# A DLRM tower on one core: a memset behind each gather, no pause for the dots, dense features turned in the third pass, loads in a new order

## The reference

```python
e = jnp.stack([tbl_0[ids[:, 0]], ..., tbl_25[ids[:, 25]]], axis=1)      # [512, 26, 128]
combined = jnp.concatenate([dense_features[:, None, :], sparse_features], axis=1)
interactions = jnp.einsum('bnd,bmd->bnm', combined, combined)
z = jnp.concatenate([dense_features, interactions[:, _TRIU_I, _TRIU_J]], axis=1)
h = jnp.concatenate([z, r_dense_features], axis=1)                      # 607 columns
h = jnp.maximum(h @ W_top1 + b_top1, 0.0)                               # 512
h = jnp.maximum(h @ W_top2 + b_top2, 0.0)                               # 256
y = h @ W_top3
```

## Time and profile before

| what | value |
|---|---|
| median of 3 runs | 134.91 us |
| time of the profiled execution | 134.64 us |
| its span in the profile | 132.1 us |
| TensorE busy | 110.6 us (84%) |
| VectorE busy | 83.8 us (63%) |
| ScalarE busy | 77.6 us (59%) |
| GpSimd busy | 59.6 us (45%) |

### The profile page before, as it was taken

The page is one execution under the profiler, slowest core; times in us unless marked ns, Lnnn a source line. Parts: engine busy times, 40 slices in busy tenths (PEclk is TensorE's granted clock), DMA queues, the critical chain, the costliest instruction groups (busy, mean ns, idle before and its releaser), DMA issues.

```text
span 132.1 us, 2612 instructions
## 1 busy us (share of the span) xinstructions
PE 110.6 (84%) x1036; PEld 94.5 (72%) x1036; DVE 83.8 (63%) x161; ACT 77.6 (59%) x146; POOL 59.6 (45%) x57
## 2 busy tenths in 40 slices
PE   0032996999999999999999189949989997999992
PEld 0022654868888888888888099849978996899891
DVE  5422399999999998897932507954950683095101
ACT  3019972499795959598584307945960776067120
POOL 2087878879788979878778400004700000000000
PEclk9999999999999999999999855999999999999999
DMA  4999976939888785881211100000110000000000
GB/s 96 275 406 390 347 264 186 297 118 212 342 207 330 202 336 191 261 314 56 56 48 46 53 0 5 0 5 7 52 25 0 5 0 0 5 0 5 0 0 1
DMA packets 6492, 16.99 MB, mean 129 GB/s; under 512 B 1617, under 2 KB 2897, under 8 KB 6354
## 3 DMA queue, kind: packets, MB, share of 16 engines
q1 hardware_dynamic: 4274, 13.38, 29.5%
q0 software_dynamic: 1536, 3.15, 8.7%
q10 hardware_dynamic: 672, 0.32, 1.0%
HBM read 16.83 MB, written 0.00 MB: 127 GB/s over the span
## 4 chain that ended last, share of the span: by engine, by line
POOL 41%; PE 25%; issue 17%; DVE 9%; DMA 5%; ACT 2%
POOL rows L306 41%; PE dots_ps L620 8%; DVE z L324 8%; PE acc_ps L647 8%; DMA ids_sb<-ids 4%; PE turn_ps L661 3%; PE acc_ps L638 2%; PE turn_ps L593 2%; ACT z L348 1%; PE acc_ps L661 1%; PE turn_ps L671 1%; DVE cols L316 1%; PE acc_ps L671 1%; DMA rows<-tbl,ids_sb 1%; ACT h L427 0%
## 5 line engine op out<-in xcount | busy, mean ns | idle before, releaser
L306 POOL DMA_INDIRECT rows<-tbl,ids_sb x48 | 58.7, 1222 | 35.0 <-PE turn_ps L593 16.4
L465 DVE TENSOR_SCALAR onehot<-ids_row,row_number 128x1024 fp32r<-128x1024 int32 x49 | 33.2, 745 | 4.3 <-PE acc_ps L568 3.1
L324 DVE COPY z<-dots_ps 30x128 f32<-30x128 f32 (+5 forms) x80 | 21.0, 263 | 8.8 <-issue 5.6
L348 ACT ACTIVATE z<-dots_ps 30x128 f32<-30x128 f32 (+5 forms) x80 | 19.7, 246 | 11.5 <-PE dots_ps L620 10.3
L620 PE MATMUL dots_ps<-cols 128*64 128x52 f32 x512 | 18.9, 240 | 6.3 <-DMA rows<-tbl,ids_sb 3.2
L620 PEld LDWEIGHTS dots_ps<-cols 128*64 128x64 f32 x512 | 18.2, 156 | 7.5 <-issue 5.6
L560 PE MATMUL acc_ps<-onehot,table_hi 128*128 128x512 f32 x68 | 18.7, 422 | 3.1 <-ACT table_hi L348 3.1
L475 DVE TENSOR_TENSOR table_lo<-table_raw,table_hi 128x2048 fp32r<-128x2048 f32 (+1 forms) x8 | 16.6, 2079 | 4.8 <-ACT table_hi L348 4.8
L560 PEld LDWEIGHTS acc_ps<-onehot,table_hi 128*128 128x128 f32 x68 | 13.0, 200 | 8.3 <-ACT table_hi L348 4.2
L568 PE MATMUL acc_ps<-onehot,table_lo 128*128 128x512 f32 x68 | 17.4, 408 | 1.0 <-DVE table_lo L475 1.0
L348 ACT ACTIVATE cols<-turn_ps 128x512 f32<-128x512 f32 x10 | 10.6, 1082 | 10.4 <-PE turn_ps L593 10.4
(11 more groups left out here) (42 smaller groups left out, 72.0 us busy)
## 6 DMA issues: line engine op xcount, KB each, us to landing
table_raw<-picked_tables SPq DMA_DIRECT2D x14, 512.0 KB, 7.0
ids_row<-ids_picked SPq DMA_DIRECT2D x7, 512.0 KB, 5.1
table_raw<-w SPq DMA_DIRECT2D x1, 1536.0 KB, 8.4
rows<-tbl,ids_sb POOLq DMA_INDIRECT x48, 3.7
w_sb<-w SPq DMA_DIRECT2D x1, 512.0 KB, 12.5
dense_sb<-dense ACTq DMA_DIRECT2D x1, 256.0 KB, 6.8
table_raw<-picked_tables SPq DMA_DIRECT2D x2, 128.0 KB, 5.8
ids_sb<-ids ACTq DMA_DIRECT2D x1, 52.0 KB, 5.3
```

The lines of the kernel that those rows point to most:

```text
L306: nc.gpsimd.indirect_dma_start(rows[:, t % GATHER_RING, n, :], None, tables[f][:, :], index).then_inc(rows_in[t][g], 16)
L324: last = copy(z[QUAD * q:QUAD * q + rows_of, t % 2, :, QUAD * s + b0:QUAD * s + b1], src.rearrange("i b c -> i c b"))
L348: return nc.scalar.activation(dst, src, ACT.Copy)
L465: nc.vector.tensor_scalar(onehot[:, c], ids_row[:, pair % IDS_RING], row_number[first_row][:, c:c + 1], None, ALU.is_equal).then_inc(oneho ...
```

## The change

- Behind each of the 48 gathers GpSimd clears `breath`, 256 columns of 128 partitions that nobody reads. The memset of gather k waits for that of gather k-1.
- `PAUSES` and `LANDED` are empty: group (3,2) is no longer held back until the dots of tile 1 are done, and `dots(0)` waits for no landing.
- The dense features are turned between the two halves of pass 2 (`DENSE_PASS`), and their three copies stand in passes 3, 4 and 5 of ScalarE. ScalarE's first instruction on data is now `split_hi(0)`; the one-hot of pass 1 is made ahead of `split_hi(1)`.
- `dense_sb` is loaded by SP, behind the tables of pass 2, from an array laid out on the host so that a partition's data is contiguous; so is `w2`; `w3` and `b2` are one load.
- In the tiles t >= 1, group (t+2, 2) is turned behind layer 2, and moved by ScalarE behind `activate2`.

```diff
-PAUSES = {(3, 2): 1}
-LANDED_FIRST = [(3, 0), (3, 1)]
+DENSE_PASS = 2
+PAUSES = {}
+LANDED = {}
+BREATH = 256
...
-            for p in range(PASS_RING):
-                if PASSES[p][3] and PASSES[p][0] < IDS_RING:
-                    load_ids_row(PASSES[p][0])
-                load_tables(p)
-            sp.dma_start(w2_sb[:], w2.rearrange("(k p) o -> p k o", p=P)).then_inc(w2_in, 16)
-            sp.dma_start(w3_sb[:], w3).then_inc(small_in, 16)
-            sp.dma_start(b2_sb[:], b2).then_inc(small_in, 16)
+            load_ids_row(0)
+            load_tables(0)
+            load_tables(1)
+            load_ids_row(1)
+            load_tables(2)
+            sp.dma_start(dense_sb[:], dense).then_inc(dense_in, 16)
+            sp.dma_start(w2_sb[:], w2).then_inc(w2_in, 16)
+            sp.dma_start(last_sb[:], last_weights).then_inc(small_in, 16)
...
                     for n in group:
                         f = GATHERED[n]
+                        k = t * len(GATHERED) + n
                         index = bass.IndirectOffsetOnAxis(ap=ids_sb[:, t, f:f + 1].bitcast(U32), axis=0)
                         nc.gpsimd.indirect_dma_start(rows[:, t % GATHER_RING, n, :], None, tables[f][:, :],
                                                      index).then_inc(rows_in[t][g], 16)
+                        if k:
+                            pool.wait_ge(breathed, k)
+                        nc.gpsimd.memset(breath[:], 0.0).then_inc(breathed, 1)
...
-            act.wait_ge(dense_turned, 1)
-            copy(dense_t[:].rearrange("d (h e j) -> d h e j", e=2, j=QUAD),
-                 dense_turned_ps.rearrange("d (h j e) -> d h e j", e=2, j=QUAD))
-            copy(cols[:, :, 0], dense_turned_ps)
-            copy(cols[:, :, NODES + REPEATS.index(0)], dense_turned_ps).then_inc(dense_moved, 1)
             split_hi(0)
-            for p in range(NP):
-                if ACT_CHUNKS[p]:
+            measure(1)
+            finish_onehot(1)
+            split_hi(1)
+            for p in range(1, NP):
+                if p >= 2:
                     measure(p)
                 if p + 1 < NP:
                     split_hi(p + 1)
-                if ACT_CHUNKS[p]:
+                if p >= 2:
                     finish_onehot(p)
...
+                if p - DENSE_PASS in (1, 2, 3):
+                    move_dense(p - DENSE_PASS - 1)
...
                 activate1(t)
-                for g in range(2, NG):
-                    move_group(t + 2, g)
+                if t == 0:
+                    for g in range(2, NG):
+                        move_group(t + 2, g)
                 if t + 1 < TILES:
                     evacuate(t + 1, 0, 2)
                 activate2(t)
+                if t >= 1:
+                    for g in range(2, NG):
+                        move_group(t + 2, g)
...
                 last.then_inc(hi_used, 1)
+                if p == DENSE_PASS:
+                    turn_dense()
...
-                    for u, g in LANDED_FIRST:
-                        pe.wait_ge(rows_in[u][g], 16 * len(GROUPS[g]))
+                for u, g in LANDED.get(t, ()):
+                    pe.wait_ge(rows_in[u][g], 16 * len(GROUPS[g]))
...
                 layer1(t, range(H1_ACT))
+                layer1(t, (H1_ACT,))
+                layer2(t)
                 for g in range(2, NG):
                     turn(t + 2, g)
-                layer1(t, (H1_ACT,))
-                layer2(t)
```

More of the change, by code:

```diff
@@ L144, in pieces_before, with build @@
     return sum(len(pieces_of(u)) for u in range(t))
-def build(nc, dense, ids, ids_picked, picked_tables, tables, w1, w2, w3, b2, out):
+def build(nc, dense, ids, ids_picked, picked_tables, tables, w1, w2, last_weights, out):
     with ExitStack() as ctx:
@@ L205, in build @@
         ids_in = sem("ids_in")
+        breathed = sem("breathed")
         ids_row_in = [sem(f"ids_row_in{i}") for i in range(IDS_RING)]
@@ L388, in move_group, with move_dense @@
                 move_turned("scalar", act.wait_ge, copy, t, g)
-            act.wait_ge(dense_turned, 1)
-            dense_turned_ps = turn_ps[0][:].rearrange("d t b -> d (t b)")
-            copy(dense_t[:].rearrange("d (h e j) -> d h e j", e=2, j=QUAD),
-                 dense_turned_ps.rearrange("d (h j e) -> d h e j", e=2, j=QUAD))
-            copy(cols[:, :, 0], dense_turned_ps)
-            copy(cols[:, :, NODES + REPEATS.index(0)], dense_turned_ps).then_inc(dense_moved, 1)
-            split_hi(0)
-            for p in range(NP):
-                if ACT_CHUNKS[p]:
+            def move_dense(part):
+                turned_ps = turn_ps[0][:].rearrange("d t b -> d (t b)")
+                if part == 0:
+                    act.wait_ge(dense_turned, 1)
+                    copy(dense_t[:].rearrange("d (h e j) -> d h e j", e=2, j=QUAD),
+                         turned_ps.rearrange("d (h j e) -> d h e j", e=2, j=QUAD)).then_inc(dense_moved, 1)
+                else:
+                    slot = 0 if part == 1 else NODES + REPEATS.index(0)
+                    copy(cols[:, :, slot], turned_ps).then_inc(dense_moved, 1)
+            split_hi(0)
+            measure(1)
[3 more added lines that the diff above has]
+                if p >= 2:
                     measure(p)
@@ L401, in _ @@
                     split_hi(p + 1)
-                if ACT_CHUNKS[p]:
+                if p >= 2:
                     finish_onehot(p)
-                if p >= 1:
-                    for t, g in PICK_TURNS.get(p - 1, ()):
-                        move_group(t, g)
-                    if PASSES[p - 1][4]:
-                        move_picked(PASSES[p - 1][0])
+                for t, g in PICK_TURNS.get(p - 1, ()):
+                    move_group(t, g)
+                if PASSES[p - 1][4]:
+                    move_picked(PASSES[p - 1][0])
+                if p - DENSE_PASS in (1, 2, 3):
+                    move_dense(p - DENSE_PASS - 1)
             for t, g in PICK_TURNS.get(NP - 1, ()):
@@ L579, in pick, with turn_dense @@
                         last.then_inc(last_done, 1)
+            def turn_dense():
+                pe.wait_ge(dense_in, 16)
+                for t in range(TILES):
+                    last = nc.tensor.transpose(turn_ps[0][:, t, :], dense_sb[:, t, :], identity[:])
+                last.then_inc(dense_turned, 1)
             def turn(t, g):
@@ L675, in _ @@
             pe.wait_ge(identity_ready, 1)
-            pe.wait_ge(dense_in, 16)
-            for t in range(TILES):
-                last = nc.tensor.transpose(turn_ps[0][:, t, :], dense_sb[:, t, :], identity[:])
-            last.then_inc(dense_turned, 1)
             for p in range(NP):
@@ L741 @@
     build(nc,
-          declare("dense", np.asarray(inputs["r_dense_features"])[order]),
+          declare("dense", np.asarray(inputs["r_dense_features"])[order].reshape(TILES, P, DIM).transpose(1, 0, 2)),
           declare("ids", ids.reshape(TILES, P, NUM_TABLES).transpose(1, 0, 2)),
```

22 lines of the change are left out of this document (11 added, 11 removed).

## The result

| | before | after |
|---|---|---|
| median of the runs taken side by side | 135.07 us (133.58 to 136.35) | 142.7 us (141.82 to 143.91) |
| profiled execution, its span | 134.64 us, 132.1 us | 141.82 us, 139.9 us |
| mean granted clock of TensorE | 0.974 | 0.939 |

The change makes the kernel slower: the ratio to the kernel before is 1.061, with a 95% interval of 1.048 to 1.074. It lies 13.7 us above the forecast of 129.0 and 9.2 above the end of the range.

A forecast was written before the change was run, and what follows sets the result against it. TensorE was taken as full in picking, and the end of dots(0)'s first piece as setting all later time. Terms of -6.25 and +0.6 took the span from 132.1 to 126.45, time 129.0 us; range 125.5 to 133.5.

The forecast's parts named there:

- gathers beside the dots: Gathers running beside dots and copies to z: 0 to 1 us for each tile, taken as 0.
- something not seen before: Rival: gathers beside the dots cost 1 to 3 us, giving 130 to 132 us; chance 0.09.
- One wait, written there: Before dots(0): only this wait, 3.18 us, once, depends on the last gather's landing, so gathers as such are no bound.
- The clock: At dots(0): without the gap the clock stays up, first piece 2.08 us instead of 3.75; -1.7 us.
- No wait for the landing: Before dots(0): it starts without waiting for the last gathers to land; -3.2 us.
- The start: With dense features moved away, TensorE's first product starts at 8.3 instead of 12.27 us; -4.0, between -3.5 and -4.4.
- Dense features in pass 2: Four transposes on TensorE in picking's pass 2, ScalarE's copies hidden; +0.6 us, between 0 and 1.1.
- The memsets: In picking they hold back VectorE's one-hots, passes 1 to 4 losing about 0.45 us each; +1.6, between 0 and 3.
- Gathers in time: Late gathers of tile 3: the 44th lands at 96.7 us, wanted at 96.1; +0.6 us.
- The turn of (3,2): Turned behind layer 2, it makes the dots of tile 3 start at 111.45 us; +0.45, between 0 and 1.
- The signs that the forecast named: Wrong if TensorE waits over 2 us for rows, first product waits for a load until 10, or clock falls elsewhere.

The follow-up runs named there:

- e13: Changed kernel with memsets, of 512 columns, only behind the 12 gathers of tile 3; 124.55 us, ratio 0.935 to the kernel before.
- e3: Kernel before, without the pause ahead of group (3,2) and without the landing wait of dots(0), no memsets; 137.45 us, ratio 1.009.
- e8: e1 with table_lo made in four instructions and dots(0) waiting for the landing of all of tile 3; 157.92 us, ratio 1.154.
- e7: e5 with 24 plain loads of 64 KB from SP's queue added beside dots(0); 133.94 us, one execution.
- e11: e5 with 12 plain loads of 64 KB from GpSimd's own queue added beside dots(0); 131.18 us, one execution.
- e1: Changed kernel with all 48 memsets left out; 135.46 us, ratio 0.997 to the kernel before.
- e5: e1 with a pause ahead of group (3,1) until the dots of tile 1 are done, no landing wait; 133.15 us, ratio 0.980.
- e9: Changed kernel with memsets, of 256 columns, only behind the 12 gathers of tile 3; 135.64 us, ratio 0.997 to the kernel before.
- e10: Changed kernel with memsets, of 1024 columns, only behind the 12 gathers of tile 3; 125.27 us, ratio 0.920 to the kernel before.

## Why the prediction was wrong

`e13` lets the forecast's steps be measured without the stall: from `dots(0)` on it is the kernel that the forecast describes, but for longer memsets behind its gathers, and from VectorE's last copy to the end it takes 44.84 us, as after does. After is 17.5 us longer than `e13` in span: 4.95 up to the start of `dots(0)` (72.64 against 67.69), 6.07 to the first copy, 6.48 in the copies.

**The step that failed: gathers beside the dots.** The forecast said that there is no row for it, gave 0 to 1 us for each tile, and took 0, since the transposes of picking ran beside gathers at their usual pace. It costs 6.07 + 6.48 = 12.55 us. As its own rival ("something not seen before") it had 1 to 3 us and 0.09: the mechanism was on the list, its size was off by a factor of four at least. The argument by the transposes was the fault. The row it went by is 1.03 us long, and the stall takes longer to show: in `e3` the same transposes take 1.03 us at 71.96, beside the same gathers, and the dots stall from 74.5. Through most of picking the gathers were being slowed by VectorE (a `table_lo` in every pass, and one-hots in between), which is what `e8` takes away, and there picking stops too. Free gathers came in before only in short rows, of two or three from 66.83 and from 70.93 and of four from 90.73, with no stall that its rows show; behind the second row TensorE waited for the landing. "One wait, written there" was read as a cost alone. The Trainium skill, "SBUF — State Buffer", section "SBUF: two separate sides", says that DMA and engines use separate ports, that a transfer can't be slowed by a compute operation or the other way round, and that TensorE never waits on anyone; a reader who goes by it takes 0 as well. For `e7`'s plain transfers these runs agree, and for `e11`'s as far as they go; beside indirect gathers 1.25 us apart TensorE does wait (23.80 us before one product in `e8`), and the measurement decides. Whether it is a port that it waits for, no run shows.

**The clock.** Forecast -1.7, for a gap that closes. The gap closed and the clock fell all the same, between 77 and 78 us, behind a microsecond in which TensorE was busy for 0.36. The term belonged to the same step: in `e13`, with no stall, it holds (first copy 2.18 us behind the start, where it was 3.75).

**No wait for the landing.** Forecast -3.2 and `dots(0)` directly behind the turns. Right: 72.64 behind turns that began at 71.67.

**The start.** Forecast -4.0, first product at 8.3. Right in kind, undersized: 6.49, so -5.78. `table_hi` started at 5.57 us, 2.3 us before the forecast had the second table land. The first two tables land a median 4.3 us behind their issue, where it was 5.8 [page, part 6]. That it is the load of dense features that had cost these first loads so much more than its share of the queue said is argued from its being the load taken away; no run put it back alone.

```profile
5.57 0.82 ACT L357 ACTIVATE table_hi<-table_raw 128x256 fp32r<-128x256 f32 x2 [3.08 <-DMA table_raw<-picked_tables]
...
6.49 2.05 PE L580 MATMUL acc_ps<-onehot,table_hi 128*128 128x512 f32 x4 [6.49 <-DVE onehot L487]
```

**Dense features in pass 2.** Forecast +0.6. From the first product to the end of picking it took 60.8 us before and 61.3 in `e1`, so +0.45 for this and all else that isn't a memset: right.

**The memsets.** Forecast +1.6 (0 to 3); with them the same stretch takes 66.2 us, +4.9. The mechanism was right. GpSimd and VectorE of after in pass 4:

```profile
37.42 1.21 POOL L313 DMA_INDIRECT rows<-tbl,ids_sb  x1 [0.16 <-issue]
38.61 0.34 POOL L317 MEMSET breath<- 128x256 f32 x1
39.11 1.21 POOL L313 DMA_INDIRECT rows<-tbl,ids_sb  x1 [0.16 <-issue]
...
42.02 0.33 POOL L317 MEMSET breath<- 128x256 f32 x1
42.51 2.37 POOL L313 DMA_INDIRECT rows<-tbl,ids_sb  x1 [0.16 <-issue]
```

```profile
36.02 5.83 DVE L487 TENSOR_SCALAR onehot<-ids_row,row_number 128x1024 fp32r<-128x1024 int32 x7
41.77 2.28 DVE L497 TENSOR_TENSOR table_lo<-table_raw,table_hi 128x2048 fp32r<-128x2048 f32 x1
```

Seven one-hots take 5.83 us where they took 4.72: three memsets of 0.34 and a little more each. The cycle is the part that was mis-sized: 1.69 us, two one-hots and a memset, instead of the 2.27 forecast (three one-hots and one). The memset ends 0.16 us ahead of the next gather, not 0.30, and the gather still catches the second boundary. More gathers a pass mean more memsets a pass: four instead of three. VectorE then needs 8.0 to 8.3 us a pass, never waits, and bounds every pass from 2 to 7, while the forecast had it in the lead only through pass 4. The Trainium skill, "SBUF — State Buffer", section "SBUF: two separate sides", calls this an exclusive lock held for a whole instruction, and restricts it, for a VectorE operation with two SBUF inputs, to GpSimd operations that read SBUF. The trace agrees with both halves: one-hots give way to the memset, and the memset of 42.02, which reads nothing, runs its usual 0.33 us beside `table_lo`, which takes its usual 2.28. In which mode the one-hots run, the profile doesn't say.

**Gathers in time.** Forecast +0.6. Nothing waited: the last gather starts at 89.47 instead of the 100 or so forecast, for the same reason.

**The turn of (3,2).** Forecast +0.45, measured +0.46 on the last interval of the first section, and all of it lies ahead of the dots of tile 3 (23.74 us behind VectorE's last copy, 23.27 before). Right; the row is their wait for ScalarE's copy.

```profile
118.80 2.08 PE L648 MATMUL dots_ps<-cols 128*64 128x52 f32 x64 [1.11 <-ACT cols L357]
```

Put together with measured sizes: -5.78 + 0.45 + 4.9 - 3.2 - 1.6 + 0.46 = -4.8 of span, 129.8 us in all with the 2.54 us around the span of before. After has 1.92 around it (141.82 - 139.9), a difference that the forecast had no term for, so 129.2; `e13` with the 4.95 us by which after reaches the dots later gives 129.3. That this is so near the forecast is luck: the errors at the start (1.8 us too little gained) and in the memsets (3.3 too little lost) cancel in part. What stands between the forecast and the result is the one step that had no row: 129.2 + 12.55 = 141.8. The signs that the forecast named did show it: the clock fell elsewhere, and the first piece did not take 2.1 us.

## What to carry to other kernels

A wait that looks needless may be what keeps two things apart; before it is priced as a gain, look whether the trace has any row in which the two run side by side undisturbed for as long as they will, and if it has none, try that one edit alone first. An engine's waits show up on its readers: where the records of an engine thin out with "issue", and even where they don't, time it by the engine that waits for it. A deliberate gap costs what it holds up: put it only where it is wanted (12 gathers, +0) and not everywhere (48 gathers, +4.9 us), and find its size by a run or two.

## What the hardware showed

Indirect gathers (128 rows of 512 bytes, 0.94 us of GpSimd each) that follow each other every 1.25 us, with 0.30 us between them, all but stop TensorE: 1 to 3 records per 1.4 us in the dots of `e1`, and a picking that stands still for over 22 us in `e8`. With one every 1.45 us some 4 records (`e9`) to 8 (after) get through per gather, with one every 1.65 all. It shows some 4 to 8 us behind the first gather of a row that nothing holds up (after: 70.69, records thin out from 74.6; `e5`: 82.21 and 87.3; `e8`: 15.70, and VectorE waits from 23.6); how soon differs, and at the start of `e1` nine gathers, one every 1.35 us (4.97 to 15.79), pass without it. It ends 0.7 us (after) to 4.2 us (`e8`) behind the end of the last one. VectorE and ScalarE are not slowed: their 16 copies in after take 3.82 us, as half of 7.68 before.

What lies between the gathers and TensorE stays open. It isn't the clock, which falls behind the stall; nor the amount of data, 76 GB/s in `e8` against 271 in picking; nor the loading of instructions as far as the trace shows it: between 0 and 60 us `e8` has no packet on the instruction queues, so TensorE went on at 56.76 without one. The next stands in the DMA queues of `e8` within 60 to 61 us (packets, MB, share):

```profile
q8 instruction: 1, 0.02, 6.8%
```

Whether TensorE works slower or only its signals reach the other engines late is open as well. The thinned records (`e1`, `e9`) speak for the first, records ahead of the readers by 3 us and more (after, `e8`) for the second.

Nor was it tried whether gathers with other row lengths, or a plain load repeated for longer than 6.5 us from GpSimd's queue, do the same. In `e10` the 128 records of `dots(0)` take 0.33 us more than in `e13` although its gathers are further apart; no run explains that.

A memset on GpSimd took 0.33 us for 256 fp32 columns of 128 partitions, 0.54 for 512 and 0.97 for 1024.
